# Gated pass of a graph network on one core: edge terms of two batches in one step, ring of turned attributes from six pairs to eight

## The reference

```python
# layer 0, for every edge
msg_in   = concat([h[src], h[dst], e64])                 # 128 + 128 + 64
messages = (silu(msg_in @ w1 + b1) @ w2 + b2) * sigmoid(msg_in @ wg + bg)
agg      = segment_sum(messages, dst)
# layer 2, for every edge and each of its two attention layers
a_e      = edge_attr_128 @ We @ att_e                    # the "edge term"
```

## Time and profile before

| | |
|---|---|
| median of 3 runs | 1939.49 us (1938.94 to 1941.75) |
| the profiled execution | 1941.41 us, span 1939.5 us |
| busy | PE 1623.6 us (84%), DVE 1463.3 us (75%), ACT 1049.4 us (54%), POOL 937.0 us (48%) |
| gated pass in the span | first pair's turn at 63.48 us, last pair's at 642.7 us, last sum at 657 us |

### The profile page before, as it was taken

How to read it: one execution, slowest core, us unless ns; L and a number is a source line. 1 busy time by engine, 2 the same in 40 slices (tenths; PEclk the granted TensorE clock), 3 DMA queues, 4 the chain that set the end, 5 groups by cost and what they waited for, 6 DMA issues and landing times. The chain is left out here.

```text
span 1939.5 us, 44470 instructions
## 1 busy us (share of the span) xinstructions
PE 1623.6 (84%) x13670; PEld 1310.2 (68%) x13670; DVE 1463.3 (75%) x4393; ACT 1049.4 (54%) x2866; POOL 937.0 (48%) x940
## 2 busy tenths in 40 slices
PE   6699999999999749998556988956588887499996
PEld 5588888888887616556455877856477777266664
DVE  5688888888887698996668888856888886644656
ACT  2577677776776366773306878830377785311000
POOL 4777777777776120000455777535667773200000
PEclk9799999999999859999755999976589998699998
DMA  6888788888887002333552111127121112254442
GB/s 197 251 268 244 243 261 245 258 264 259 260 247 238 11 5 80 126 126 126 161 111 53 42 41 42 36 62 193 40 59 40 42 41 86 86 194 173 171 170 91
DMA packets 148931, 273.61 MB, mean 141 GB/s; under 512 B 28039, under 2 KB 88909, under 8 KB 146436
## 3 DMA queue, kind: packets, MB, share of 16 engines
q1 hardware_dynamic: 110430, 192.44, 30.3%
q0 software_dynamic: 33408, 75.68, 14.6%
q10 hardware_dynamic: 4854, 2.55, 0.5%
HBM read 225.06 MB, written 45.51 MB: 140 GB/s over the span
## 5 line engine op out<-in xcount | busy, mean ns | idle before, releaser
L997 POOL DMA_INDIRECT gated_rows<-p_tab,src_idx x416 | 436.8, 1050 | 150.3 <-issue 124.9
L1405 POOL DMA_INDIRECT cur<-table,src_idx x240 | 245.3, 1022 | 105.9 <-issue 49.4
L2260 PE MATMUL bank<-counts,mean_xs 128*128 128x416 bf16 (+2 forms) x1350 | 220.4, 322 | 32.0 <-DVE mean_xs L1762 32.0
L1593 PE MATMUL bank<-attention_counts,h_sb 128*128 128x260 f32 (+1 forms) x900 | 216.4, 363 | 13.8 <-ACT attention_counts L1548 9.9
L1526 ACT ACTIVATE attention_lo<-attention_plain,w_left 128x128 fp32r<-128x128 bf16 x512 | 176.7, 394 | 87.1 <-DVE attention_plain L1640 87.0
L1038 PE MATMUL bank<-gated_wide_q,gated_comb 128*128 128x256 f32 x832 | 216.0, 382 | 0.0
L1114 ACT ACTIVATE gated_sig<-gated_pre 128x512 f32<-128x512 f32 x208 | 131.4, 632 | 152.9 <-DVE gated_pre L1202 145.6
L2260 PEld LDWEIGHTS bank<-counts,mean_xs 128*128 128x128 bf16 x1350 | 126.4, 98 | 116.8 <-issue 35.4
L1202 DVE TENSOR_TENSOR gated_pre<-bank,gated_rows 128x512 f32<-128x512 f32 x208 | 142.8, 687 | 79.3 <-PE bank L1038 79.3
L1576 PE MATMUL bank<-attention_wide_a,attention_lo 128*128 128x300 f32 x512 | 151.7, 380 | 46.0 <-issue 31.8
L1593 PEld LDWEIGHTS bank<-attention_counts,h_sb 128*128 128x128 f32 x900 | 146.8, 191 | 26.2 <-ACT attention_counts L1548 17.4
(11 more groups left out here) (450 smaller groups left out, 3983.2 us busy)
## 6 DMA issues: line engine op xcount, KB each, us to landing
counts<-count_tabs SPq DMA_DIRECT2D x16, 2675.0 KB, 9.8
h_sb<-in_edge_attr_dram SPq DMA_DIRECT2D x51, 512.0 KB
count_tabs<-mean_counts SPq DMA_DIRECT2D x40, 535.0 KB, 2.7
gated_relr<-rel_rows SPq DMA_DIRECT2D x104, 128.0 KB
gated_ids<-id_rows SPq DMA_DIRECT2D x26, 512.0 KB
gated_wide_q<-q_tab SPq DMA_DIRECT2D x208, 64.0 KB
attend_hot_lo<-low_hots SPq DMA_DIRECT2D x52, 256.0 KB
gated_ea<-in_edge_attr_dram SPq DMA_DIRECT2D x51, 256.0 KB
```

Source lines behind the costliest of these rows:

```text
L997: pool.indirect_dma_start(out=rows[:, q % TICKS, c, :], out_offset=None, in_=p_tab, in_offset=bass.IndirectOffsetOnAxis(ap=src_idx[:, b, j ...
L1405: pool.indirect_dma_start(out=ring_row(n, j), out_offset=None, in_=table, in_offset=bass.IndirectOffsetOnAxis(ap=src_idx[:, gathered_batch ...
L1593: mm = pe.matmul(BANKS_D[k % 2][:, 0:width], h_sb[:, m, :], counts[:, home(first), m, at:at + width], start=(m == 0), stop=(m == NT - 1), ...
L2260: mm = pe.matmul(BANKS_D[q % ND][:, 0:width], xs[l][:, m // 3, m % 3, :], counts[:, s % 2, m // 3, at:at + width], start=(m == 0), stop=(m ...
```

## The change

The terms of two batches (`TERMS` = 2) are made together, at the last pair of the second batch, so at every fourth pair instead of every second. Sixteen matmul instructions in a row then take the place of twice eight; the second batch's go to the columns `3P:4P` of the bank. One copy of 256 columns takes the place of two copies of 128. The ring of turned attributes is eight pairs deep, so that the attributes of both batches are still there, and the scalar engine's wait before it overwrites a place in the ring is for the group of four pairs that used it last. The semaphore of the copies counts once for two batches.

```diff
-            TRN = 6
+            TRN, TERMS = 8, 2
@@
+            assert AG_ % TERMS == 0 and NB % AG_ == 0
@@ keep_edge_terms
-                        sp.wait_ge(ae_placed, (g + 1) * AG_)
+                        sp.wait_ge(ae_placed, (g + 1) * AG_ // TERMS)
@@ turn_silu
-                        if k == PAIRS - 1:
-                            for j in range(J):
-                                pe.matmul(ST[j * AE_COLS:(j + 1) * AE_COLS, 2 * P:3 * P], ae_v[:, :], eaT[:, (q - k + j // 2) % TRN, j % 2, :],
-                                          start=True, stop=True, skip_group_check=True)
+                        if (q + 1) % (TERMS * PAIRS) == 0:
+                            for i in range(TERMS):
+                                for j in range(J):
+                                    pe.matmul(ST[j * AE_COLS:(j + 1) * AE_COLS, (2 + i) * P:(3 + i) * P], ae_v[:, :],
+                                              eaT[:, (q + 1 - (TERMS - i) * PAIRS + j // 2) % TRN, j % 2, :],
+                                              start=True, stop=True, skip_group_check=True)
@@ place_eaT
-                        reach(act, s_turned, q - TRN + 2)
+                        reach(act, s_turned, ((q - TRN) // (TERMS * PAIRS) + 1) * TERMS * PAIRS)
@@ copy_siluT
-                        if k == PAIRS - 1:
+                        if (q + 1) % (TERMS * PAIRS) == 0:
                             reach(act, ae_kept[b // AG_ % 2], 32 * (b // AG_ // 2))
-                            act.copy(ae_rows[:, b // AG_ % 2, b % AG_, :], ST[:, 2 * P:3 * P]).then_inc(ae_placed, 1)
+                            first = b % AG_ + 1 - TERMS
+                            act.copy(flat(ae_rows[:, b // AG_ % 2, first:first + TERMS, :]), ST[:, 2 * P:(2 + TERMS) * P]).then_inc(ae_placed, 1)
```

## The result

The changed kernel takes 1920.12 us (median of 4 runs, 1918.98 to 1920.3) against 1939.22 us of the kernel before in the same job: a ratio of 0.9903, 95% interval 0.9888 to 0.9918. In two later jobs it came out at 0.9907 (0.9878 to 0.9936) and 0.9921 (0.9907 to 0.9934) of the kernel before. So the gain is 15 to 19 us, 0.8 to 1.0%. The prediction was 1925.1 us, a gain of 14.4 us, in a range of 1918.5 to 1935.0; the first median lies 1.6 us inside the fast end of that range.

What follows compares the result with a forecast made beforehand. The prediction took PE's instruction list to bound the gated pass. Savings of 12.5 us (joined groups) and 2.5 us (pair after the looks), less 0.4 and 0.2 at the ends, gave 14.4 us: 1939.49 to 1925.1 us, range 1918.5 to 1935.0.

Steps and rivals of the forecast that it cites:

- What bounds the kernel: Gated pass: PE's own instruction list sets the pace; terms cost 0.51 us of it for every batch.
- the slower rival: Odd pairs keep 2.96 us through the ACT, DVE, PE chain; 13.5 us slower, 1953 us; chance 0.05.
- The rival of the transfers: Loads whose start depends on PE land late and give the whole gain back: 1939.5 us; chance 0.08.
- Part 1: Sixteen term matmuls in one go save 0.24 us for two batches, 52 times: 12.5 us (bounds 6.8 and 15.1).
- The rival by which later rounds wait for their weights: Each later round of term matmuls costs 0.06 us more: gain about 8 us, 1931.5 us; chance 0.14.
- Part 2: Pair after the looks: stall shrinks from 0.34 to 0.19 us in some 17 groups of eight, 2.5 us.
- Part 3: ACT's 52 fewer copies, three bare pairs in a row and the ring's new wait cost nothing.
- Part 4: POOL, 21.8 us for eight pairs, falls behind PE by 0.45 us, but its 7-pair lead lasts; PE never waits for rows.
- Part 5: Ends of the pass: 0.4 us saved before pair 204 vanishes in PE's wait; another 0.2 us lost at the first pairs.
- The sum: Whole kernel: 12.5 + 2.5 - 0.4 - 0.2 = 14.4 us gained, 1925.1 us for the median.

Runs made afterwards that it cites:

- the terms at the other place: Changed kernel with terms of four batches at once from pair 75, made at pairs 7 modulo 8, not ahead of the pair after the looks: 1924.06 us, ratio 0.9911.

## Why the prediction was right, and where it wasn't

**What bounds the kernel.** Right. PE's own list sets the pace before and after; the bare odd pairs came out at 2.45 us each, so the slower rival (odd pairs keep their 2.96 us) is refuted. The rival of the transfers is too: at a DMA share of 0.88 the pairs keep their rhythm, and the pass gave its gain.

**Part 1, the price of a group.** The mechanism is right, its size was a little low. The four sizes of group that were run give one formula: 0.49 us with two rounds (four instructions), 0.51 with two (eight), 0.73 with four, 3.61 - 2.45 = 1.16 with eight. That is about 0.29 us fixed and 0.11 us for each round. The prediction took 0.13 us for a later round, from the distance between the two rounds that there were; 0.11, its other bound, was right. The trace of the changed kernel has 0.133 us from the first round to the second and 0.109 from then on, so the first distance is longer; why is not shown. The saving is 2 x 0.51 - 0.73 = 0.29 us for two batches, 52 x 0.29 = 15.1 us instead of 12.5. This term was mis-sized, by 2.6 us. The rival by which later rounds wait for their weights had half of it: the third set of loads does start only with the second round of matmuls. But its price, 0.19 us for a round, is refuted by the same 0.11.

**Part 2, the pair after the looks.** The chain was the right one; the stall went to 0.25, not to 0.19 us. Nearly all of the difference follows from part 1: PE arrives 0.22 us later, not 0.27. The chain behind the looks grew by 0.13 us (from the start of the pair before to the matmul L1054 it is 4.62 us instead of 4.49), where the prediction had 0.12 for the copy alone: the wide copy is 0.10 of it, and the looks' first instruction took 0.09 us longer (1.36 instead of 1.27) but began 0.07 us earlier in its pair. 0.34 - 0.22 + 0.13 is 0.25 us, and with that the gain is 17 x 0.09 = 1.5 us in place of 2.5. The kernels without looks, without terms, and with the terms at the other place (stalls of 0, 0.89 and 0.69 us) show the same chain from three sides.

**Part 3, the copies and the ring.** Right as far as the runs can tell: the ring alone left the length of those 17 groups of eight as it was, and two copies in place of one cost 1.0 us in them.

**Part 4, POOL.** This step failed, and the forecast was none the worse for it, since by this step too PE set the pace to the end. It took POOL's 21.8 us for eight pairs as its own, fixed pace and had it fall behind by 0.45 us in eight. It didn't; it needed 16 x (1.006 + 0.30) = 20.9 us and still waited for DVE. How long a gather needs to land, which the prediction left open, is in the trace's record of the semaphores: in the kernel before, 5.3 us from the start of a pair's second call as a rule and at most 8.2 (pairs 72 to 199), so the 11 us were enough. The long call beside the looks depends on where it meets them. The timelines of POOL, before and after:

```profile
306.60 2.30 POOL L997 DMA_INDIRECT gated_rows<-p_tab,src_idx  x1 [0.30 <-issue]
```

```profile
299.32 1.55 POOL L998 DMA_INDIRECT gated_rows<-p_tab,src_idx  x1 [0.30 <-issue]
```

The first began 0.28 us after the looks and the second 0.61 us after them. 23 of 416 calls took over 2.1 us before and 5 after. The other half of the step, that the lead of 7 pairs is used up first and PE waits only then, is what the kernel without terms shows: nearly ten groups of eight at 20.5 us, then waits for rows.

**Part 5, the ends.** Right: PE's idle before pair 204 grew from 5.27 to 5.76 us, and what was saved just before it vanished (timeline of PE):

```profile
616.21 0.44 PE L1026 MATMUL bank<-ident,gated_ea 128*128 128x128 f32 x1 [5.76 <-issue]
```

**The sum.** 15.1 + 1.5 less about 1 us at the ends is close to the 15.5 us by which the pass shrank in the first pair of profiles; the forecast was 14.4. By stretches, the 16 groups before pair 64 should give 4.6 us (measured 4.2), the 17 groups of eight up to pair 200 should give 34 x 0.29 + 1.5 = 11.4 (measured 11.3), and the last pairs gave nothing, since what they save is lost again before pair 204. The 19.1 us between the medians of the first job are more than these steps explain. The other jobs have 18.7 and 16.7, and what is above 15.5 is not traced to a place. So the forecast is right in its steps, and that the first median came so near the fast end of the range is partly chance.

## What to carry to other kernels

Count the switches of a matmul's shape before the matmuls: a group of narrow ones costs a fixed price that is only paid once when groups are joined, and the price can be read from two neighbouring pairs, one with and one without. Before such a group is made larger or moved, look at what it covers where it stands, and walk through every queue that waits for its result: a store in the load queue turned a gain of 7 us into a loss of 30. Here the distance between two rounds was too long for the third, so keep the plain pace of such an instruction in the range as well. And before a difference of a few us is booked to an edit, take it from a stretch that repeats.

## What the runs showed of the hardware

- Sixteen matmul instructions on four column tiles of 32 start in four rounds, 0.13 us from the first to the second and 0.11 us from then on; 32 last 1.08 us. A load of 32 columns in f32 lasts 0.11 us, eight begin within 0.05 us, and the third set of four begins when the second round of matmuls starts. The order in which the program names the tiles changed a group of 0.64 us by 0.03.
- A GpSimd gather call takes 0.94 us at its shortest. Beside the vector engine's looks (1.27 us, bf16 to fp8, and 0.56 us) it took 2.30 us when it began 0.28 us after them, and 1.55 when it began 0.61 after them; in the second case the call before it, begun 0.8 us ahead of the looks, took 1.12. Without the looks the long calls were gone. The vector engine's instruction itself took 1.27 us in the first case and 1.36 in the second.
- In the 13 profiled executions that leave the ring of gathered rows alone, the part outside the pass took 1354.5 to 1361.5 us, 0.5% from least to most. A single profiled execution is not enough to book 5 us to an edit. The whole pass repeated to 0.6 us in three profiles of the changed kernel, and to 2.0 us in the two kernels with the groups of before; pairs 64 to 199 repeated to 0.1 us.
